# One head's K projection, moved into the chunk loop of the head before: a transformer layer on eight cores

## The reference, cut to what matters

```python
x = x + attn(layernorm(x), Wq, Wk, Wv, Wo, rms_w)      # x: 4 x 2048 x 2048
x = x + ffn(layernorm(x), W1, W2, W3)

# attn: q, k, v = x @ Wq, x @ Wk, x @ Wv in 16 heads of 128; q, k rotated
# linear attention with decay, in chunks of 128 tokens, a 128 x 128 state kv per head:
def step(kv, (qi, ki, vi)):
    inter = (qi * q_decay) @ kv
    intra = ((qi @ ki.T) * dmask) @ vi
    kv_new = r_C * kv + (ki * k_decay).T @ vi
    return kv_new, inter + intra
# then rms norm, @ Wo
# ffn: W2 @ fwht(silu(W1 x) * (W3 x)), hidden size 8192
```

## Time and profile before

| | us |
|---|---|
| median of 2 runs | 3868.38 (3866.41 to 3870.35) |
| the profiled execution, as timed | 3869.86 |
| its span, slowest core (core 5) | 3868.3 |
| spans of the eight cores | 3850.5 to 3868.3 |

### The profile page before, as it was taken

The page is one execution under the profiler, slowest core; times in us unless marked ns, Lnnn a source line. Parts: engine busy times, 40 slices in busy tenths (PEclk is TensorE's granted clock), DMA queues, the critical chain, the costliest instruction groups (busy, mean ns, idle before and its releaser), DMA issues.

```text
span 3868.3 us, 33677 instructions; the slowest of 8 cores (3850.5 to 3868.3 us)
## 1 busy us (share of the span) xinstructions
PE 2569.3 (66%) x11196; PEld 1088.2 (28%) x11196; DVE 971.3 (25%) x1312; ACT 1011.7 (26%) x1594; POOL 8.8 (0%) x20
## 2 busy tenths in 40 slices
PE   3355565567997222235577688788688785289888
PEld 0022222213443111111231233333233332134333
DVE  0412211123112444452222321322322223600000
ACT  1112212211112444422102233333233332023222
POOL 0000000000000000000000000000000000000000
PEclk9677777788998555557798899999899998699999
DMA  5322112114553110111241233334234342045453
GB/s 160 125 76 66 57 53 66 33 44 157 191 191 114 40 36 33 33 42 38 93 158 54 66 131 131 110 131 130 87 131 131 109 131 98 33 148 168 163 173 132
DMA packets 124218, 392.51 MB, mean 101 GB/s; under 512 B 12432, under 2 KB 12688, under 8 KB 115600
## 3 DMA queue, kind: packets, MB, share of 16 engines
q1 hardware_dynamic: 107920, 348.41, 27.2%
q10 hardware_dynamic: 13824, 33.56, 2.4%
q0 software_dynamic: 2304, 8.39, 0.7%
HBM read 356.76 MB, written 33.55 MB: 101 GB/s over the span
## 4 chain that ended last, share of the span: by engine, by line
PE 63%; DVE 18%; ACT 8%; issue 6%; DMA 4%; DVEq 1%; ACTq 1%; SPq 0%
PE p L1034 11%; PE pg L928 11%; PE pl L940 11%; PE psumP L596 9%; PE ppj L419 7%; PE psumW L835 3%; DVE hid L975 2%; DVE hid L978 2%; DVE htmp L953 2%; PE p_sx_ln L505 1%; PE p_sx_ln L511 1%; ACT ktp L452 1%; ACT ktil L696 1%; DVE scrA L543 1%; DVE actA L545 1%
## 5 line engine op out<-in xcount | busy, mean ns | idle before, releaser
L1034 PE MATMUL p<-hid,wb 128*128 128x512 bf16 x2048 | 451.6, 384 | 150.4 <-DVE hid L978 102.4
L928 PE MATMUL pg<-actA,wb 128*128 128x512 bf16 x2048 | 459.0, 383 | 43.0 <-DVE actA L545 43.0
L940 PE MATMUL pl<-actA,wb 128*128 128x512 bf16 x2048 | 452.5, 379 | 0.0
L596 PE MATMUL psumP<-actA,wbf 128*128 128x512 bf16 x1536 | 333.6, 380 | 44.3 <-DVE wbf L587 44.3
L1034 PEld LDWEIGHTS p<-hid,wb 128*128 128x128 bf16 x2048 | 201.9, 99 | 400.1 <-issue 164.8
L419 PE MATMUL ppj<-xlnp,wbfp 128*128 128x512 bf16 x1024 | 258.7, 417 | 81.3 <-DVE wbfp L413 60.2
L928 PEld LDWEIGHTS pg<-actA,wb 128*128 128x128 bf16 x2048 | 201.9, 99 | 292.1 <-issue 54.9
L940 PEld LDWEIGHTS pl<-actA,wb 128*128 128x128 bf16 x2048 | 200.4, 98 | 241.7
L953 DVE TENSOR_TENSOR htmp<-gsil,pl 128x1024 bf16<-128x1024 bf16 x64 | 78.2, 1221 | 745.2 <-PE pl L940 744.9
L1023 ACT ACTIVATE wb<-land 128x1024 bf16<-128x1024 f32 x128 | 135.2, 1057 | 454.1 <-PE p L1034 328.5
L966 ACT ACTIVATE hid<-pg 128x1024 bf16<-128x1024 f32 x64 | 65.5, 1023 | 580.2 <-PE pg L959 580.2
(11 more groups left out here) (134 smaller groups left out, 2026.5 us busy)
## 6 DMA issues: line engine op xcount, KB each, us to landing
land<-w_t SPq DMA_DIRECT2D x384, 512.0 KB, 5.4
preland<-xp SPq DMA_DIRECT2D x32, 512.0 KB, 4.0
preland<-wk_t SPq DMA_DIRECT2D x32, 512.0 KB, 4.4
preland<-wv_t SPq DMA_DIRECT2D x32, 512.0 KB, 4.6
wland<-wq_t SPq DMA_DIRECT2D x16, 1024.0 KB, 5.2
wland<-wk_t SPq DMA_DIRECT2D x16, 1024.0 KB, 5.0
wland<-wv_t SPq DMA_DIRECT2D x16, 1024.0 KB, 5.1
wland<-wo_t SPq DMA_DIRECT2D x16, 1024.0 KB, 6.0
```

What stands on the lines that cost most here:

```text
L596: pe_val = p.emit("pe", lambda e, par=par, k=k, half=half: e.matmul(psumP[par][:, half * 512:(half + 1) * 512], wbf[par][:, k * 128:(k + 1 ...
L928: w1_pe = p.emit("pe", lambda e, par=par, k=k, half=half: e.matmul(pg[par][:, half * 512:(half + 1) * 512], wb1[par][:, k * 128:(k + 1) * ...
L940: w13_pe = p.emit("pe", lambda e, par=par, k=k, half=half: e.matmul(pl[par][:, half * 512:(half + 1) * 512], wb3[par][:, k * 128:(k + 1) * ...
L1034: "pe", lambda e, par=par, cc=cc, m4=m4, half=half, hs=hs, c=c: e.matmul(p8[m4][:, half * 512:(half + 1) * 512], wb1[par][:, cc * 512 + m4 ...
```

## The change

The loop over heads is rearranged. `feed_tile` (load), `cast_tile` (cast) and `mm_emitter` (the 32 matmuls in eight groups of four) take the place of the inner loop over K and V. K of head 0 is computed ahead of the loop. In head h, the K tile of head h+1 is loaded and cast after the rotation, and its eight groups of matmuls are emitted one in each chunk, on PE between the two transposes and L459. The copy of K to `kpbuf` stands at the start of the next head. In the q projection the waits of the casts and of the first matmul are written in another way.

```diff
+    def mm_emitter(wpar, cval):
+        for j0 in range(0, 32, 4):
+            def grp(j0=j0, wpar=wpar, cval=cval):
+                mmv = None
+                for j in range(j0, j0 + 4):
+                    k, half = j // 2, j % 2
                     mmv = p.emit("pe", lambda e, k=k, half=half, wpar=wpar: e.matmul(
                         ppj[:, half * 512:(half + 1) * 512],
                         wbfp[wpar][:, k * 128:(k + 1) * 128],
                         xlnp[:, k * T + half * 512: k * T + (half + 1) * 512],
                         start=(k == 0), stop=(k == 15)),
+                        waits=([("dve", max(cval, nrm_done)), ("act", last_ev)]
+                               if j == j0 == 0 else ()),
+                        inc=("pe" if j == 31 else None))
+                return mmv
+            yield grp
+
+    g0 = feed_tile(wk_h, 0, 0, 0)
+    cast_of[(0, 0)] = cast_tile(g0, 0)
+    mm_end = None
+    for grp in mm_emitter(0, cast_of[(0, 0)]):
+        mm_end = grp()
+    wl_rd[0] = mm_end
+    for h in range(NH):
+        ev_kp = p.emit("act", lambda e: e.activation(out=kpbuf[:, :], in_=ppj[:, :], func=AF.Copy),
+                       waits=[("pe", wl_rd[0])], inc="act")
+        last_ev = ev_kp
+        gv = feed_tile(wv_h, h, 1, 1)
+        cast_of[(h, 1)] = cast_tile(gv, 1)
+        mm_end = None
+        for grp in mm_emitter(1, cast_of[(h, 1)]):
+            mm_end = grp()
+        wl_rd[1] = mm_end
+        ev_vp = p.emit("act", lambda e: e.activation(out=vpbuf[:, :], in_=ppj[:, :], func=AF.Copy),
+                       waits=[("pe", wl_rd[1])], inc="act")
+        last_ev = ev_vp
...
         krotp = p.emit("dve", lambda e: e.tensor_add(kp_rot[:, :], scrA[:, :], scrB[:, :]), inc="dve")
+        grps = None
+        if h + 1 < NH:
+            gk = feed_tile(wk_h, h + 1, 0, 0)
+            cast_of[(h + 1, 0)] = cast_tile(gk, 0)
+            grps = list(mm_emitter(0, cast_of[(h + 1, 0)]))
         av = None
+        mm_end = wl_rd.get(0, 0)
         for c in range(NCH):
...
             t2v = p.emit("pe", lambda e, cs=cs, pT2=pT2: e.transpose(pT2[:, :], vpbuf[:, cs],
                                                                      idents[:, :]),
                          waits=[("act", prev_vtp[ce])], inc="pe")
+            if grps is not None:
+                mm_end = grps[c]()
...
             cast_val[gi] = p.emit(
                 "dve", lambda e, par=par: e.tensor_copy(wbf[par][:, :], wland[par][:, :]),
-                waits=[(f"d_w{par}", 16 * (gi // 2 + 1)),
-                       ("dve", p05_dve_end if gi < 2 else 0),
-                       ("act", s7_done if gi < 2 else 0),
-                       ("pe", pe_proj.get(gi - 2, p05_pe_end))], inc="dve")
-            mm_waits = [("dve", max(cast_val[gi], ln1_done)), ("act", evac_val.get(gi - 2, 0))]
+                waits=[(f"d_w{par}", 16 * (gi // 2 + 1)), ("dve", ln1_done),
+                       ("pe", pe_proj.get(gi - 2, 0))], inc="dve")
+            mm_waits = [("dve", cast_val[gi]), ("act", evac_val.get(gi - 2, 0))]
```

More of the change, by code:

```diff
@@ L403, in build_program, with feed_tile, cast_tile @@
     dp_cnt = 32
[L404 to L418, removed]
+    cast_of = {}
+    def feed_tile(wt_h, h, wpar, wsel):
+        nonlocal prev_cast, dp_cnt
+        for half in range(2):
+            p.dma("sp", preland[half][:, :], wt_h.ap()[h][:, half * 1024:(half + 1) * 1024],
+                  waits=[("dve", prev_cast), ("dve", nrm_done)], inc=f"d_p{half}")
+        gen = dp_cnt // 2 + 1
+        dp_cnt += 2
+        return gen
+    def cast_tile(gen, wpar):
+        nonlocal prev_cast
+        for half in range(2):
+            prev_cast = p.emit("dve", lambda e, half=half, wpar=wpar: e.tensor_copy(
+                wbfp[wpar][:, half * 1024:(half + 1) * 1024], preland[half][:, :]),
+                waits=[(f"d_p{half}", 16 * gen), ("pe", wl_rd.get(wpar, 0))], inc="dve")
+        return prev_cast
+    def mm_emitter(wpar, cval):
[4 more added lines that the diff above has]
+                    k, half = j // 2, j % 2
                     mmv = p.emit("pe", lambda e, k=k, half=half, wpar=wpar: e.matmul(
@@ L423, in build_program @@
                         start=(k == 0), stop=(k == 15)),
[L424 to L431, removed]
+                        waits=([("dve", max(cval, nrm_done)), ("act", last_ev)]
[22 more added lines that the diff above has]
+        last_ev = ev_vp
         p.emit("pe", lambda e: e.matmul(pp_rot[:, 0:512], PTs[:, :], kpbuf[:, 0:512],
                                         start=True, stop=True),
-               waits=[("act", ev), ("dve", prev_m2p), ("d_c", dc_all)])
+               waits=[("act", ev_vp), ("dve", prev_m2p), ("d_c", dc_all)])
         prot = p.emit("pe", lambda e: e.matmul(pp_rot[:, 512:1024], PTs[:, :], kpbuf[:, 512:1024],
```

## The result

| us | before | after |
|---|---|---|
| undisturbed executions | 3866 to 3874 | 3784 to 3787 |
| profiled execution, span of the slowest core | 3868.3 (core 5) | 3783.8 (core 3) |
| spans of the eight cores | 3850.5 to 3868.3 | 3765.5 to 3783.8 |
| ratio, 95% interval | | 0.9779 (0.9764 to 0.9795) |

The kernel is faster by 2.2%, about 85 us, at some 3785 us; forecast were 78 us and 3790. The medians over all timed executions are 3944.7 before and 3906.7 after, the latter outside the forecast range: seven of the changed kernel's eleven had a mean TensorE clock of 0.749 to 0.820 on one or both dies where the other four had 0.835 to 0.840, and the long executions of the kernel before, beside the later runs, had 0.737 to 0.815 where its short ones had 0.825 to 0.828; the ratio above, and all that follows, compares the short ones.

The account below looks back on a forecast made before the run. The partner's-heads stage was taken as a chain of handovers with no engine full. Per head 8.60 saved, less 1.9 for the loop and 1.5 for V, gives 5.2 us; 15 heads, 78 us: 3868 to 3790 us, range 3758 to 3815.

Parts of the forecast that it names:

- handover ahead of V: Between the last L459 and V: S7g, then the kpbuf copy, PE idle 1.95 us per head, covered by nothing.
- chunk 1: Second chunk of the loop, at the low clock: 1.96 us against 1.51, +0.45 per head.
- chunk 2: Third chunk of the loop, only a little of it at the low clock: +0.2, with 0 and 0.45 as ends.
- warm chunks: Chunks 2 to 7 at the high clock: steps of 1.40 us instead of 1.51, -0.65 per head; bounds 1.51 and 1.30.
- The bound: Stage of the partner's heads, 573.6 us: no engine full, a chain of handovers; what it loses, the kernel loses.
- What was removed: K block of heads 1 to 15 with its gaps: 0.13 + 9.10 + 1.32 = 10.55 us per head.
- Chunk 0's lost cover: First chunk: PE waits for the next K tile's cast until 1.6 us after loop start; L459 at 3.3, +1.9 us.
- The low chunks: Loop's start: low clock lasts 4.1 us, covering chunks 0 and 1 and a little of chunk 2.
- V after the gap: V projection after the longer idle gap: price 0 or 1.3 to 1.7 us; 1.5 taken. Rival, no fall: 3768 us, chance 0.20.
- In nearly all heads or in nearly none: V blocks: the clock falls in nearly every head or hardly any, because the heads' pattern repeats.
- The q projection's waits: Rewritten cast and matmul waits in the q projection: cost nothing, gain nothing.
- Loads: K tile lands in 4.5 us, first used some 20 us later; V's weights ready too; both stay hidden.

Follow-up runs that it names:

- the overlap undone: Changed kernel with the eight groups of K matmuls put in a row behind the last chunk's L459; head 35.76 us on core 0, time 3879.5 us.
- the early cast: Changed kernel with the load and cast of the next K tile put ahead of the rotation; 3758 us, head 28.37 us.
- the rotation filled: Changed kernel with 16 extra matmuls behind the rotation's two in heads 0 to 14; 3762 us, head 29.01 us.
- the own accumulator: Changed kernel with K given an accumulator ppk of its own, so V no longer waits for the kpbuf copy; 3737 us, head 27.30 us.
- the filler: Changed kernel with eight extra matmuls behind the last L494, in the gap ahead of V, heads 0 to 14; 3765 us, head 28.93 us.
- the run with every second chunk empty: Changed kernel with own K accumulator, early K load and cast, 16 K matmuls in the rotation, 16 in every second chunk; 3734 to 3747 us, ratio 0.9664.
- the last version: Changed kernel with own K accumulator, early K load and cast, 8 K matmuls behind the rotation's two, 3 per chunk; 3698 us, ratio 0.9555.

## Why the prediction was right or wrong, point by point

The terms of the sum, per head, with what this head and the run that isolates it measured:

| term | forecast | measured |
|---|---|---|
| handover ahead of V | 1.95 | 1.90 |
| chunk 0, first transpose to L459/L494 | 3.3 | 3.25 |
| chunk 1 | 1.96 | 2.03 |
| chunk 2 | 1.60 (1.40 to 1.85) | 1.74, mean 1.64 |
| warm chunks | 1.40 | 1.36 |
| V block | 7.07 + 1.5 | 8.6 to 8.75 in 14 of 15 heads |
| head | 30.6 | 30.38 |
| 15 heads | 78 | 80.9 |

- *The step that failed* is the one that takes the baseline: "against a median of 3868.4, so the sum goes against the same number: 3868 - 78 = 3790 us". Two executions, both near 3868, stood for the kernel's time, and the range of 3758 to 3815 had no term for how far executions of one kernel lie apart: it was put at nothing, without a reason. The runs showed it to be larger than the change. Ten executions of the kernel before took 3866 to 4264 us, with a median of 3944.7, and eleven of the changed one 3784 to 4151, with a median of 3906.7, outside the range. The medians lie 38 us apart, not 78. A better baseline alone would not have mended it: 3944.7 - 78 is 3867, still 40 us off. The sum itself, against executions like the two that it was taken from, holds: 3784 to 3787 us.
- *The bound.* A chain of handovers in this stage, worth what it loses: the 80.9 us of the stage arrived at the end in full (81.9 at the feed-forward layer's start, 84.5 in the span).
- *What was removed.* With the overlap undone all of it came back, so the 10.55 us of the K block and its gap were the right thing to count.
- *Chunk 0's lost cover.* Right: PE stands until 1.59 us after the first transpose (forecast 1.6), 1.22 us of waiting, which the early cast takes away. *The low chunks*: right in size, though the sum counts chunk 2 among the warm six as well. I put them down to a clock that stays low from the idle rotation; with the rotation filled, chunk 1, behind the wait for the cast, still took 1.70 to 2.03 us in 10 of 15 heads.
- *V after the gap.* The term I was least sure of, 0 or 1.3 to 1.7, came at 1.6 to 1.7 in 14 of 15 heads and at 0 in one. "In nearly all heads or in nearly none" was right for this kernel and no general rule: with the early cast it was ten heads of 15. The reason that I gave, the sparse work ahead of the gap, isn't shown. Without the idle gap (0.28 us with the own accumulator, eight matmuls in it with the filler) V took 7.07 us in all 15 heads, but no run changed the loop's filling with the gap left alone; and since the same gap behind a loop filled the same gives V blocks of both lengths, the two together don't decide it. That it came in 14 of 15 heads here was in part luck.
- *The clock in the loop.* The transposes of the old loop took 0.27 or 0.31 us at a clock of 0.50; in the new one those from chunk 3 on ran warm, at 0.22 us. The full loop then stayed at 1.00 through its last five chunks, 413.35 to 420.11 us. In the run with every second chunk empty the clock was at 0.50 from chunk 4 into V (420.30 to 428.00 us).
- *The rest.* The q projection's waits: nothing, as said. Loads: never late. Where the terms are off is small: 0.04 in each of the warm steps, and 2.7 us at the end of the feed-forward layer for which I have no cause.

## What to carry to other kernels

Where an in-order engine stands between short operations of another, put a long independent job into the gaps in equal pieces, small enough to be hidden, and look at TensorE's clock: here, with four or three matmuls in every chunk, in the changed kernel and the last version, the last four chunks of a head took 1.36 us each in 14 of 15 heads and had one step of 1.64 or 1.65, at a clock of 1.00, in the other; with four in every second chunk they took 1.55 to 1.98 in 14 of 15 heads, at 0.50 in the one shown. When a block moves, look at what it covered (here the cast) and at what now waits for its result (here a shared accumulator): the two took 4.8 of the 30.4 us that a head still had. A handful of matmuls whose result nobody reads is a cheap probe for what the clock costs.

## What the runs showed of the hardware that I had not expected

- In the changed kernel the clock fell after the gap was over, while TensorE was busy without a break: the gap ahead of V (420.40 to 422.00 us) and V's first us were at 1.00, V's third us (424.00 to 425.00) at 0.50, and V as a whole (422.01 to 430.76) at a mean of 0.80.
- In the run with the overlap undone two cores of one die differed: over 204.6 to 219.0 us core 3 had a mean clock of 0.81 and core 0 one of 1.00. Core 3's first V block took 8.56 us, core 0's 7.07.
- With the early cast, V blocks of 7.07 us (351.19, clock 1.00) and of 8.75 us (378.66, clock 0.80) stood behind the same gap of 1.69 us and a loop filled the same. No run shows what decided it.
